# Ranking the edges of a graph layer in three parts, with marks and weight remainders moved to GpSimd

## What is computed

```python
xn = layernorm(x)
h = xn @ gnn_W                                       # 625 x 768
deg = segment_sum(1, dst); s = rsqrt(deg)            # with a loop on every node
gnn = segment_sum(h[src] * (s[src] * s[dst])[:, None], dst) + gnn_b
mix = linear_attention(xn @ W_qkv, proj_mat) @ W_proj + b_proj
x = x + gnn + mix
x = x + experts(layernorm(x))                        # 16 experts, fc1 768x1536, fc2 1536x768
```

## Time and profile before

| | us |
|---|---|
| median of 3 runs | 1185.01 |
| lowest, highest | 1183.92, 1187.00 |
| the profiled execution's own time | 1186.22 |
| its span, first to last instruction | 1184.5 |
| TensorE busy in it | 1135.8 |
| VectorE, ScalarE, GpSimd busy | 753.8, 656.7, 481.6 |
| mean granted TensorE clock, share of full | 0.986 |

### The profile page before, as it was taken

How to read it: one execution, slowest core, us unless ns; L and a number is a source line. 1 busy time by engine, 2 the same in 40 slices (tenths; PEclk the granted TensorE clock), 3 DMA queues, 4 the chain that set the end, 5 groups by cost and what they waited for, 6 DMA issues and landing times.

```text
span 1184.5 us, 20975 instructions
## 1 busy us (share of the span) xinstructions
PE 1135.8 (96%) x6492; PEld 1004.5 (85%) x6493; DVE 753.8 (64%) x1154; ACT 656.7 (55%) x1040; POOL 481.6 (41%) x392
## 2 busy tenths in 40 slices
PE   5999999999999999999999999999999999999985
PEld 5999998788565778889999988888889999998874
DVE  7951643464677375525966865747775896665973
ACT  3222673264400163346786685847777878387953
POOL 1388888888602000542222322314443273123721
PEclk9999999999999999999999999999999999999998
DMA  9030005321201230156687565565786958378933
GB/s 313 21 92 2 3 3 143 122 73 27 74 1 29 93 121 13 27 174 213 227 316 252 212 244 183 179 226 191 286 292 221 355 197 329 107 260 301 363 101 94
DMA packets 62960, 191.85 MB, mean 162 GB/s; under 512 B 13867, under 2 KB 15206, under 8 KB 62916
## 3 DMA queue, kind: packets, MB, share of 16 engines
q1 hardware_dynamic: 51188, 173.01, 39.8%
q0 software_dynamic: 11728, 18.27, 8.7%
HBM read 178.81 MB, written 15.16 MB: 164 GB/s over the span
## 4 chain that ended last, share of the span: by engine, by line
PE 82%; DVE 6%; ACT 5%; issue 2%; DMA 2%; ACTq 0%; SPq 0%; DVEq 0%; POOL 0%; POOLq 0%
PE banks L1976 26%; PE banks L1956 25%; PE banks L1691 5%; PE banks L1708 4%; PE banks L1856 3%; PE banks L1926 3%; PE banks L1878 3%; PE banks L1780 2%; PE banks L1758 2%; PE banks L1723 2%; PE banks L1919 2%; ACT kfeat L1451 2%; ACT kfeat L1446 1%; PE banks L1933 1%; PE banks L1840 1%
## 5 line engine op out<-in xcount | busy, mean ns | idle before, releaser
L737 POOL DMA_INDIRECT edge_dram<-epair,eslot x165 | 219.1, 1328 | 92.1 <-issue 91.8
L814 POOL DMA_INDIRECT out<-ysb,sidx x27 | 109.2, 4044 | 217.4 <-issue 210.5
L522 ACT ACTIVATE w2hi<-w2raw 128x1536 fp32r<-128x1536 f32 x96 | 139.2, 1483 | 92.5 <-DMA w2raw<-in_L_ffn_fc_w 82.2
L535 DVE TENSOR_TENSOR w2lo<-w2raw,w2hi 128x1536 fp32r<-128x1536 f32 x96 | 164.5, 1751 | 23.6 <-ACT w2hi L522 20.8
L1976 PE MATMUL banks<-w2hi,hthi 128*128 128x384 f32 x624 | 162.2, 341 | 0.2 <-DVE htlo L1230 0.2
L1976 PE MATMUL banks<-w2lo,hthi 128*128 128x384 f32 x624 | 159.5, 336 | 0.0
L1976 PE MATMUL banks<-w2hi,htlo 128*128 128x384 f32 x624 | 159.3, 336 | 0.0
L522 ACT ACTIVATE w1hi<-w1raw 128x1536 fp32r<-128x1536 f32 x96 | 137.5, 1498 | 27.2 <-DMA w1raw<-in_L_ffn_fc_w 25.3
L1956 PE MATMUL banks<-w1hi,xthi 128*128 128x512 f32 x486 | 139.5, 395 | 1.7 <-POOL w1lo L535 1.7
L535 DVE TENSOR_TENSOR w1lo<-w1raw,w1hi 128x1536 fp32r<-128x1536 f32 x80 | 138.2, 1789 | 0.0
L1956 PE MATMUL banks<-w1lo,xthi 128*128 128x512 f32 x486 | 136.9, 390 | 0.0
(11 more groups left out here) (345 smaller groups left out, 1891.1 us busy)
## 6 DMA issues: line engine op xcount, KB each, us to landing
w1raw<-in_L_ffn_fc_w SPq DMA_DIRECT2D x96, 768.0 KB, 6.6
w2raw<-in_L_ffn_fc_w SPq DMA_DIRECT2D x96, 768.0 KB, 6.3
xs<-in_x SPq DMA_DIRECT2D x10, 336.0 KB
edge_dram<-epair,eslot POOLq DMA_INDIRECT x165, 2.6
wg<-in_L_gnn_W SPq DMA_DIRECT2D x1, 2304.0 KB, 12.2
wv<-in_L_mix_W_qkv SPq DMA_DIRECT2D x1, 2304.0 KB, 13.7
wk<-in_L_mix_W_qkv SPq DMA_DIRECT2D x1, 2304.0 KB, 17.6
wq<-in_L_mix_W_qkv SPq DMA_DIRECT2D x1, 2304.0 KB, 10.4
```

The costliest lines, as they stand in the source:

```text
L522: act.activation(unit(w2hi if second else w1hi, second, u), unit(w2raw if second else w1raw, second, u), ACT.Copy).then_inc(w2_hi if secon ...
L535: eng.tensor_tensor(unit(w2lo if second else w1lo, second, u), unit(w2raw if second else w1raw, second, u), unit(w2hi if second else w1hi, ...
L737: pool.indirect_dma_start(out=edge_dram, out_offset=bass.IndirectOffsetOnAxis(ap=eslot[:, k:k + 1], axis=0), in_=epair[:, k, :].bitcast(I3 ...
L814: pool.indirect_dma_start(out=out, out_offset=bass.IndirectOffsetOnAxis(ap=sidx[:, 0:1], axis=0), in_=ysb[:, :], in_offset=None, bounds_ch ...
```

## The change

1. Edges are marked, scanned and ranked part by part, in parts of 33, 66 and 66 columns (28, 68 and 69 before). VectorE marks the first part alone (25 instructions of 33 columns), GpSimd the other two (25 of 2x66), at its start.
2. The bucket totals, which the first place needs, come from 10 products on TensorE over the marks (`bucket_counts`), placed ahead of the products "h", and not from the scan; each part has its own `bucket_ranks` (after "h" 0, "h" 4 and "v" 0).
3. The remainder of ("h", 0) is made by GpSimd in two pieces of 3 chunks, not by VectorE in one.
4. `lt` and `pt` go to PSUM banks 0 and 1 and ahead of the last two turns of `xt`.
5. Counts are woven into n = 4, 5, 6 of the projection, after every chunk. VectorE waits for the edge table after the first `add_projection`, and makes one or two batches of one-hots ahead of each of the next.
6. All six remainders of w1's first expert are made by GpSimd, right behind its last indirect write; VectorE makes none.

The diff, cut to its core:

```diff
-PARTS_OF_EDGES = [(0, 28), (28, 96), (96, ET)]
+PARTS_OF_EDGES = [(0, 33), (33, 99), (99, ET)]
+TOGETHER = 20
...
-FIRST_BESIDE, LAST_BESIDE = 5, 8
+FIRST_BESIDE, LAST_BESIDE = 4, 7
...
-def beside(n, third):
-
-    return ET_TILES * (3 * (n - FIRST_BESIDE) + third) // (3 * (LAST_BESIDE - FIRST_BESIDE))
+def beside(n, c):
+
+    done = 15 if c == C else 2 * c
+    return ET_TILES * (15 * (n - FIRST_BESIDE) + done) // (15 * (LAST_BESIDE - FIRST_BESIDE))
...
-        groups([("lt", 0)], R3)
-        groups([("pt", 0)], R3)
+        groups([("lt", 0)], [0])
+        groups([("pt", 0)], [1])
+        groups([("et", 0)], [2])
+        groups([("er", 0)], [3])
+        groups([("er", 1)], [4])
+        groups([("er", 2)], [3])
...
-            groups([("pj", n // 2, n % 2)], [6 if n in (1, 3) else 2 if n == 2 * NT - 1 else 7])
+            groups([("pj", n // 2, n % 2)], [6 if n in (1, 3) else 0 if n == 2 * NT - 2 else 2 if n == 2 * NT - 1 else 7])
...
+            pool.wait_ge(ebucket_ok, 1)
+            a, b, two_parts = PARTS_OF_EDGES[1][0], PARTS_OF_EDGES[1][1], ehot[:, BUCKETS * PARTS_OF_EDGES[1][0]:]
+            for n in range(BUCKETS):
+                last = pool.tensor_scalar(two_parts.rearrange("p (u b k) -> p u b k", u=2, b=BUCKETS)[:, :, n, :],
+                                          ebucket[:, a:ET].rearrange("p (u k) -> p u k", u=2), float(n), None, ALU.is_equal)
+            last.then_inc(marks_ok, 1)
+            pool.wait_ge(half_hi, 1)
+            for c in (0, 3):
+                pool.tensor_tensor(wlow["h"][:, c:c + 3, 0:384], wraw["h"][:, c:c + 3, 0:384],
+                                   high_half("h", 0)[:, c:c + 3, :].bitcast(F32), ALU.subtract).then_inc(half_lo_pool, 1)
...
-            split_lo(pool, False, 0, range(C))
+            for u in range(C):
+                pool.wait_ge(w1_hi, u + 1)
+                pool.tensor_tensor(w1lo[:, u, :], w1raw[:, u, :], w1hi[:, u, :].bitcast(F32),
+                                   ALU.subtract).then_inc(w1_lo_pool if pools(False, u) else w1_lo, 1)
...
-            def run(a, b):
-
-                hot = ehot[:, a:b, :].rearrange("p b k -> p (b k)")
-                return dve.tensor_tensor_scan(erun[:, a:b, :].rearrange("p b k -> p (b k)"),
-                                              ones[0:TP, 0:1].broadcast_to([TP, (b - a) * ET]), hot,
-                                              0.0 if a == 0 else erun[:, a - 1, ET - 1:ET], ALU.mult, ALU.add)
-
-            def bucket_totals():
-
-                link(dve.tensor_copy(elast[:, :], erun[:, :, ET - 1]))
+                    last = dve.tensor_scalar(of_part(ehot, 0)[:, b, :], ebucket[:, 0:PARTS_OF_EDGES[0][1]], float(b), None, ALU.is_equal)
+                last.then_inc(first_marks_ok, 1)
+                dve.wait_ge(first_marks_ok, 1)
+
+            def run(n):
+
+                a, b = PARTS_OF_EDGES[n]
+                link(dve.tensor_tensor_scan(erun[:, BUCKETS * a:BUCKETS * b], ones[0:TP, 0:1].broadcast_to([TP, BUCKETS * (b - a)]),
+                                            ehot[:, BUCKETS * a:BUCKETS * b], 0.0, ALU.mult, ALU.add))
+                link(dve.tensor_copy(elast[:, :], of_part(erun, n)[:, :, b - a - 1]))
+                if n:
+                    taken(dve, ("er", n - 1))
                 dve.tensor_copy(etot[:, 0:1], elast[:, 0:1])
                 dve.tensor_tensor(etot[:, 1:BUCKETS], elast[:, 1:BUCKETS], elast[:, 0:BUCKETS - 1], ALU.subtract).then_inc(etot_ok, 1)
...
+            def bucket_starts():
+
+                ps = read(dve, ("et", 0))
+                emptied(dve.tensor_reduce(ecounts[:, :], ps[:, 0:TOGETHER * BUCKETS].rearrange("p (b k) -> p b k", k=TOGETHER), AX.X, ALU.add),
+                        ("et", 0))
+                taken(dve, ("et", 0))
...
+            def slots_of(n):
+
+                a, b = PARTS_OF_EDGES[n]
+                ps = read(dve, ("er", n))
+                link(dve.tensor_tensor(eshift[:, :], efrom[0:TP, :], ps[0:TP, 0:BUCKETS], ALU.add))
+                link(dve.tensor_tensor(eshift[:, 1:BUCKETS], eshift[:, 1:BUCKETS], elast[:, 0:BUCKETS - 1], ALU.subtract))
+                emptied(dve.tensor_tensor(efrom[:, :], efrom[:, :], ps[:, 32:32 + BUCKETS], ALU.add), ("er", n))
...
-            bucket_marks()
-            split_low(dve, "h", 0)
+            dve.wait_ge(ebucket_ok, 1)
+            first_marks()
             for kind, k in T8:
                 x_lower(kind, k)
-            link(run(0, BUCKETS))
-            bucket_totals()
+            run(0)
+            bucket_starts()
+            slots_of(0)
+            dve.wait_ge(marks_ok, 1)
+            run(1)
             split_low(dve, "h", 1)
-            edge_slots()
-            slots_of(*PARTS_OF_EDGES[0])
             split_low(dve, "v", 0)
-            slots_of(*PARTS_OF_EDGES[1])
-            slots_of(*PARTS_OF_EDGES[2])
+            slots_of(1)
+            run(2)
+            split_low(dve, "v", 1)
             tile_regions()
             split_biases()
-            split_low(dve, "v", 1)
+            slots_of(2)
...
-            for n in range(FIRST_BESIDE):
-                add_projection(n // 2, n % 2)
-                if n < 3:
-                    split_lo(dve, False, 0, (n + 1,))
+            add_projection(0, 0)
             dve.wait_ge(ld_edges, 16)
             dve.tensor_copy(ecode[:, 0:ET_TILES, :], etab[:, :, :]).then_inc(iota_r_ok, 1)
             dve.wait_ge(iota_r_ok, 2)
-            for batch in range(RING):
+            one_hots(0)
+            made = 1
+            for n in range(1, FIRST_BESIDE):
+                one_hots(made)
+                add_projection(n // 2, n % 2)
+                made += 1
+            for batch in range(made, RING):
                 one_hots(batch)
             made = RING
...
-            add_projection(4, 0)
+            for n in range(LAST_BESIDE, 2 * NT - 1):
+                add_projection(n // 2, n % 2)
...
-            split_lo(dve, False, 0, (4, 5))
...
+            def bucket_counts():
+
+                pe.wait_ge(first_marks_ok, 1)
+                pe.wait_ge(marks_ok, 1)
+                ps = fill(pe, ("et", 0))[:, 0:TOGETHER * BUCKETS].rearrange("p (b k) -> p b k", k=TOGETHER)
+                for n, (a, b) in enumerate(PARTS_OF_EDGES):
+                    for k in range(0, b - a, TOGETHER):
+                        wide = min(TOGETHER, b - a - k)
+                        last = pe.matmul(ps[:, :, 0:wide], onesb[:, :], of_part(ehot, n)[:, :, k:k + wide],
+                                         start=n == 0 and k == 0, stop=b == ET and k + wide == b - a)
+                filled(last, ("et", 0))
+
+            def bucket_ranks(n):
+
+                pe.wait_ge(etot_ok, n + 1)
+                ps = fill(pe, ("er", n))
+                pe.matmul(ps[0:TP, 0:BUCKETS], prefix[:, 0:TP], etot[:, :], start=True, stop=True)
+                filled(pe.matmul(ps[:, 32:32 + BUCKETS], onesb[:, :], etot[:, :], start=True, stop=True), ("er", n))
+
+            bucket_counts()
...
+                            if name == "h" and s == 0 and i == 0 and c % 3 == 0:
+                                pe.wait_ge(half_lo_pool, c // 3 + 1)
...
-            rows_times("h", {1: bucket_ranks})
-            rows_times("v")
+            rows_times("h", {0: lambda: bucket_ranks(0), 4: lambda: bucket_ranks(1)})
+            rows_times("v", {0: lambda: bucket_ranks(2)})
...
+                if n == 2 * NT - 2:
+                    pe.wait_ge(adj_ok, COUNT_BANKS)
...
-                    if FIRST_BESIDE <= n < LAST_BESIDE and c % 2:
-                        count(beside(n, c // 2), beside(n, c // 2 + 1))
+                    if FIRST_BESIDE <= n < LAST_BESIDE:
+                        count(beside(n, c), beside(n, c + 1))
```

66 lines of the change are left out of this document (31 added, 35 removed).

## The result

The changed kernel takes 1210.6 us (median of 4 runs, 1208.2 to 1211.5) against 1186.0 for the kernel before (4 runs, 1183.9 to 1190.8) on the same chip: ratio 1.0205, 95% interval 1.0181 to 1.0228. It is slower, as forecast, but by 24.6 us, where the forecast of 1196.5 stood 11.5 above the 1185.0 that it started from, and it lies outside the range of 1183 to 1200.5. Whether it is slower by more than 2%, the interval leaves open. The profiled execution took 1210.3, its span 1208.5.

What follows compares the result with a forecast made beforehand. TensorE, busy for 96% of the span, was taken to bound the kernel. Messages 11.7 us later, at 379.8, plus an unchanged 816.4 gave a span of 1196.2; with the median 0.5 above, 1196.7, stated as 1196.5; range 1183 to 1200.5.

Steps and rivals of the forecast that it cites:

- The start: Marking and ranking ahead of the edge writes: first write 9.2 us earlier; TensorE 2.7 us earlier, reaching the projection at 297.9.
- rival of slow marks: At the start, GpSimd's marks take over 0.7 us each; at 1.0 each the edges come 6 later: 1202; chance 0.04.
- The writes take 269.1 us whatever else happens: GpSimd's edge writes keep their length, so starting 9.2 us earlier they end at 306.6 instead of 315.8.
- The one who waits gets the turn: Beside GpSimd's w1 remainders, VectorE's two-SBUF-input instructions and cast alternate with them; second add through at 323.6.
- VectorE keeps its turn: Rival beside the w1 remainders: only GpSimd's first two hold VectorE, to 313.5; 1185.7 us, no change; chance 0.09.
- The likeliest case: In the counting stage VectorE is held turn by turn by GpSimd's remainders; messages 11.7 us later, 1196.5; chance 0.73.
- not held: Rival in the counting stage: GpSimd's remainders don't hold VectorE's one-hots; messages 2.2 us earlier, 1182.8; chance 0.14.
- Behind the second add: From the second add at 323.6: n = 3, clearing, 31.5 of counts plus 1.0 low clock, 13.1 to messages at 379.8.
- VectorE stays ahead: During the counts, four one-hot batches are ready and each further takes 1.13 us against 1.3 of counting.
- The direction: The whole kernel is slower, decided by GpSimd's holding of VectorE ahead of the second add; chance of slower 0.79.
- Unloading VectorE gives nothing: Taking w1's five remainders (5 x 1.75 us) off VectorE gains nothing, since TensorE did not wait for it there.

Runs made afterwards that it cites:

- c_start: The changed kernel with only the start part kept; projections, counts and w1 remainders as in the kernel before: 1186.1 us against 1184.6, ratio 1.0009.
- j_start_late: The kernel before with the new start, and VectorE's w1 remainders moved behind the projections and norms, five projections ahead of the counts: 1184.2 us against 1184.9, ratio 0.9997.
- p_one_input_gap: p_one_input with each of GpSimd's remainders of units 2 to 5 waiting for the end of the one ahead: 1203.6 us in one execution.
- p_one_input: Probe from the changed kernel: w1 units 1 to 5 start behind the first add, VectorE's one-input cast waits for unit 1: 1211.7 us in one execution.
- a_w1_vector: The changed kernel with five of the six w1 remainders back on VectorE, only unit 0 on GpSimd: 1196.0 us, ratio 1.0089.
- d_projection: The kernel before with only the new order of projections, casts and counts; start and w1 remainders essentially as before: 1194.0 us, ratio 1.0082.
- b_w1_pool: The kernel before with all six w1 remainders of the first expert on GpSimd behind the edge writes, none on VectorE: 1196.6 us, ratio 1.0108.
- q_row_begun_held: Probe from the changed kernel: GpSimd's units 1 to 5 released while VectorE works on a filler, further fillers and the cast behind it; time not comparable.

## Why the prediction was right in direction and wrong in size

- **The start.** TensorE's projection at 297.9 is the forecast to the tenth, and that is luck: up to 227 us the lead is 1.6 (TensorE's first `banks<-ident,q1a` begins at 227.13, and at 228.75 before), and the other 1.0 comes from the granted clock from 220 to 250, 1.00 here and 0.94 in the kernel before. c_start and j_start_late, at 0.94, reach the projection at 298.95 and 298.88. `eslot` came at 37.79, not 36.4: the marks at 0.62 (the forecast took 0.3, its upper bound was 0.45), so the two halves of the remainder ran to 27.67 instead of 25.6 and held the scan 1.8 us. The first write began at 39.0, not 37.5. The rival of slow marks was set at 0.7 and more; 0.62 was enough to make the first write 1.5 later.
- **"The writes take 269.1 us whatever else happens"** is the first step that failed. They took 315.7 - 39.0 = 276.7. The forecast itself moved two scans and a remainder behind the first write and never asked what they do to GpSimd there, though it had the rule for remainders. With the 1.5 of the start the last write lay at 315.7 instead of 306.6, 9.1 us later, which is 8.8 at the second add by the forecast's own turns (323.6 to 332.4, below).
- **"The one who waits gets the turn"** is the second. It was read from one place, where GpSimd's row had begun by waiting. In this row VectorE got none. The forecast had a rival in which VectorE keeps its turn, and none in which GpSimd does. With the table at 319.7 and turn by turn the second add would be through at 332.4 (cast behind the second remainder 322.9, batches 327.4 and 331.9, add 332.4); it was through at 339.0: 6.6 us. p_one_input_gap, where turns were taken, had it at 331.8 against 338.8 in p_one_input.
- **The likeliest case** (held, 1196.5) is the nearest of the four by its mechanism. By its number the rival of slow marks (1202) lies nearer, but for a cause that didn't occur: it put the marks at 1.0. The two cheap rivals (not held, 1182.8; VectorE keeps its turn, 1185.7) are out: the ports were held, and longer. The 14.1 us missed are the two steps, 8.8 + 6.6 = 15.4 at the second add, less 0.7 from there to the messages (55.5, forecast 56.2) and 2.4 behind them, plus 1.8 by which the median stands further above the span (2.1, forecast 0.3).
- **Behind the second add** the sum came out (55.5, forecast 56.2), with two errors that cancel. n = 3 took 5.6 as forecast (3.9 + 1.7). From there to the end of the clearing it took 2.1 instead of 4.9, since no remainder stood beside VectorE any more. The counts took 35.0 instead of 32.5 (31.5 and the 1.0 added for a low clock), though the granted clock was back at 1.00 from 344.7 on: "VectorE stays ahead" was wrong, as the row shows in which TensorE waits 5.0 us inside them.
```profile
L1898 PE MATMUL banks<-oh 128*125 128x125 bf16 x185 | 20.1, 242 | 5.0 <-DVE oh L1013 2.7 <-issue 2.1
```
- **The direction** was right for another reason than the forecast's. It let the holding of VectorE decide the sign (not held: 1182.8, faster). In a_w1_vector the cast isn't held (0.36) and the kernel is still slower (1.0089), and d_projection alone costs 9.4 us: the second add waits for a table that didn't come early. The first failed step alone makes the kernel slower; being held then adds the 13.8 us of the remainders.
- **"Unloading VectorE gives nothing"** left out that the remainders hold edge writes. Without them at 307 to 313 the last write ended 1.8 earlier in b_w1_pool than in the kernel before, and 2.8 earlier in j_start_late (315.8) than in c_start (318.6). In the changed kernel this can't be used while the cast waits: the move costs 0.0108 (12.8 us) in the old order and 0.0116 (13.8) in the new.

## What to carry to other kernels

An earlier start of a GpSimd queue gains nothing if the work that was cut out ahead of it comes back beside it: add up VectorE's two-input instructions under the queue, before and after. Put no row of GpSimd tensor instructions where VectorE's next instruction is on the path. Where it must be, a wait of each for the one ahead is worth a trial: in the one probe of it on a row that would have kept the ports, VectorE was in at once (0.36 instead of 13.6 us), though its cast came just ahead of GpSimd's instruction there. A turn-taking seen at one place is a row of its own history and has to be bounded by the whole row.

## What the runs showed of the hardware

- Remainders in a row on GpSimd kept the shared ports for up to 16.55 us, five in a row, against a VectorE instruction that takes 0.34; in other rows they gave them up after each. The Trainium skill ("SBUF — State Buffer", "SBUF: two separate sides") has the lock last for the whole instruction, and by that the trace agrees; here it also passed from one instruction to the same engine's next.
- VectorE does the same: in q_row_begun_held the rest of its second filler, a third and a cast ran through while a remainder waited 2.3 (329.26 to 331.6). In p_one_input_gap, where its first batch of one-hots had had to wait, it gave the ports up after each (8.63 for two batches, 1.19 each alone).
- Two SBUF inputs on VectorE hold GpSimd's indirect writes: 4.44 and 4.46 under a scan, 3.49 under a remainder, 1.19 alone; a one-input reduction of 3.28 held none.
- A GpSimd comparison of 132 16-bit columns takes 0.62 (mean of 25 in a row), as long as 277 columns of its two-input remainder (2.24 ns a column, 3441 ns for 1536): a short instruction isn't priced by the columns of a long one, as the forecast did (0.3).
